# Rows of the attention passes scaled and summed four to a slot

## The chip, the cores and the metric

The kernel runs on one core of a Trainium2 chip. The metric is the device time of one execution. Three runs of the kernel before took 3141.16, 3142.63 and 3146.46 us; the median is 3142.63 us.

## What is computed

A graph has 3125 nodes with 256 features each and 50000 edges, sorted by destination. Four layers follow each other, each added to its input and normalized:

```python
x = _layernorm(x + _L0_gnn_ref(x, src, dst, edge_weight, ...))   # weighted sum over edges, then a two-layer MLP
x = _layernorm(x + _L1_gnn_ref(x, W, att, src, dst))             # attention over edges, 4 heads of 64
x = _layernorm(x + _L2_gnn_ref(x, edge_index, ...))              # two such passes with self loops: 4 heads, then 1 head
x = _layernorm(x + _L3_gnn_ref(x, edge_index, edge_weight, ...)) # dot-product attention over edges, then a feed-forward net
```

In the attention of L1 and L2 every edge gets a logit from its source and its destination; a softmax over the edges of one destination gives weights, and the destination receives the weighted sum of the sources' projected rows:

```python
e = leaky_relu(es[src] + ed[dst])
ex = exp(e - segment_max(e, dst)[dst])
out = segment_sum(ex / segment_sum(ex, dst)[dst] * z[src], dst)
```

## The kernel before

The kernel goes over the edges five times: L0, L1, L2a (the first, four-headed pass of L2), L2b (the second, one-headed pass) and L3. The change is in L1, L2a and L2b, called the attention passes here. An edge pass has 416 steps (STEPS); a step is 128 edges that all end in one block of 128 destination nodes. 16 steps (GS) are a group, and there are 26 groups (NG).

What a step needs, and from which engine:

- GpSimd (POOL) gathers the 128 source rows of a step with an indirect DMA (line 690) into one of 48 ring slots, three groups' worth. The gather of step k waits until the step 48 before it is summed.
- ScalarE (ACT) makes the one-hot matrices M that say which edge goes to which node, four steps at a time (`spread_hots`, lines 2034 and 2038). M has 16 slots, one group's worth, so a batch of four waits until the four steps 16 before it are summed.
- TensorE (PE) picks the destination's part of the logits (`pick`, line 1756), and the group's chain begins.
- VectorE (DVE) multiplies each gathered row by its weights (`scale`, line 1294 with four heads, 1297 with one).
- PE sums the scaled rows into their nodes by a product with M (`sum_step`, line 1806) into one of four PSUM banks.
- DVE adds the bank to the nodes' sums in SBUF (`add`, line 1323). A sum step waits until the add four steps before it has freed its bank.

The chain of a group turns 16 steps of logits into weights. Its parts follow each other across engines: DVE gathers up the picks and makes logits (lines 1174 to 1187), PE turns them (1765), DVE scans them for running maxima (1208, 1212, 1218), PE folds (1772), DVE joins the steps (1232 to 1254), PE fans out (1777, 1784), DVE scans again and subtracts (1264 to 1279), ACT takes the exponential (2021, in `put_alphas`), PE turns it back (1789, in L2a and L2b also 1791), and ACT writes the weights beside the rows (2024). ACT also makes the factor by which old sums fade (`fade_open`, 2012), which DVE applies before a group's first add (1314 and 1317, with one head 1321).

The order is written out by hand. Each engine walks through slots t = 0, 1, 2, ...; group g's chain stands in the 16 slots from 16(g+1) on, called q = 0 to 15 here, so a group's weights are put at q = 14. All engines run their instructions strictly in the order of the program; semaphores make them wait for each other. Step k is scaled by DVE at slot k + 31 (SOFAR), summed by PE at k + 32, and added by DVE at k + 34. So one step of a group is scaled, summed and added in each slot of the next group's chain. In the last two groups of L1 and L2a some of the rows are scaled by ACT and POOL instead (`helper`).

After step SETTLED - 1 = 399 has been added, `scales` and the first blocks of the node work that follows (`early_blocks`) begin between the last adds.

Of the kernel before, what the change touches and what calls it, by code (L numbers as in the profile page):

```python
# [31 lines left out]
STEPS = PADDED + BLOCKS - 1  # L32
SPARTS = STEPS // G
GS = 16
NG = STEPS // GS
WAYS = 4
SOFAR = 31
# [11 lines left out]
SETTLED = TILES - 1 + EARLY  # L49
# [56 lines left out]
def build(nc, x, src, dst, edge_weight, L0_gnn_eps, L0_gnn_w1, L0_gnn_b1, L0_gnn_w2, L0_gnn_b2,  # L106
# [6 lines left out]
    with ctx:  # L113
# [411 lines left out]
        def helper(stage, k):  # L525

            if k < STEPS - HELPED or stage not in ("L1", "L2a"):
                return "vector"
            return ("vector", "scalar", "vector", "pool")[k % 4]

        def scaled_rows(stage, who, k):

            return sum(helper(stage, i) == who for i in range(k + 1))
# [299 lines left out]
        def _(dve):  # L833
# [284 lines left out]
            def residual(t):  # L1118

                if t - 8 not in RESIDUAL_AT:  # L1120
                    return
                b = RESIDUAL_AT.index(t - 8)
                dve.wait_ge(branch_made.sem, branch_made.at("T", b + 1))
                vec.tensor_tensor(at_block(X, b), PS[7][:, D:2 * D], at_block(X, b), ALU.add).then_inc(term_made.sem, 1)
                dve.wait_ge(term_made.sem, term_made.at("T", 2 * b + 1))
                vec.scalar_tensor_tensor(at_block(X, b), bias["bv"][:], at_block(nodeC, b)[:, 1:2], at_block(X, b),
                                         ALU.mult, ALU.add).then_inc(term_made.sem, 1)

            def gat_edges(stage, hops):
# [15 lines left out]
                else:  # L1145
                    ready = norms_of["gat"]
# [141 lines left out]
                def scale(k):  # L1288
                    j = k % RING[stage]
                    if k % GS == 0:  # L1290
                        dve.wait_ge(alphas_put.sem, alphas_put.at(stage, k // GS + 1))
                    if heads > 1:
                        z = ring[:, j, 0:width].rearrange("p (h f) -> p h f", h=heads)
                        ins = vec.tensor_tensor(z, z, ring[:, j, width:width + heads].unsqueeze(2)  # L1294
                                                .to_broadcast([P, heads, width // heads]), ALU.mult)
                    else:
                        ins = vec.tensor_scalar(ring[:, j, 0:width], ring[:, j, 0:width], ring[:, j, width:width + 1],
                                                None, ALU.mult)
                    ins.then_inc(row_scaled.sem, 1)
# [3 lines left out]
                def add(k):  # L1303
                    g, i = divmod(k, GS)
                    if i == 0:
                        blocks[0] = load_blocks(dve, g)
                    if k:
                        dve.wait_ge(sum_added.sem, sum_added.at(stage, k))
                    sums = ACC[:, bass.ds(blocks[0][i], 1), 0:cols].rearrange("p o c -> p (o c)")
                    if i == 0 and g:  # L1310
                        dve.wait_ge(fade_made.sem, fade_made.at(stage, g))
                        if heads > 1:
                            a = sums[:, 0:width].rearrange("p (h f) -> p h f", h=heads)
                            vec.tensor_tensor(a, a, fade[:, 0:heads].unsqueeze(2).to_broadcast([P, heads, width // heads]),
                                              ALU.mult).then_inc(sums_faded.sem, 1)
                            d = sums[:, width:width + heads]
                            vec.tensor_tensor(d, d, fade[:, 0:heads], ALU.mult).then_inc(sums_faded.sem, 1)
                            dve.wait_ge(sums_faded.sem, sums_faded.at(stage, 2 * g))
                    dve.wait_ge(step_summed.sem, step_summed.at(stage, k + 1))
                    if i == 0 and g and heads == 1:  # L1320
                        ins = vec.scalar_tensor_tensor(sums, sums, fade[:, 0:1], PS[k % SUMS[stage]][:, 0:cols], ALU.mult, ALU.add)
                    else:
                        ins = vec.tensor_tensor(sums, sums, PS[k % SUMS[stage]][:, 0:cols], ALU.add)  # L1323
                    ins.then_inc(sum_added.sem, 1)

                early_blocks = slots(0, EARLY, hops) if hops else None
                for t in range(STEPS + SOFAR + 3):
                    g, q = divmod(t - GS, GS)
                    for early in (True, False):
                        if 0 <= g < NG:  # L1330
                            logits(g, q, early)
                            inside(g, q, early)
                            across(g, q, early)
                            peaks(g, q, early)
                        if early and stage == "L3":
                            if 0 <= t - 3 < STEPS:
                                dot(t - 3)
                        elif early and 0 <= t - SOFAR < STEPS and helper(stage, t - SOFAR) == "vector":
                            scale(t - SOFAR)
                    k = t - SOFAR - 3  # L1340
                    if 0 <= k < STEPS:
                        add(k)
                        if hops and k == SETTLED - 1:
                            scales(stage, 0)
                        elif hops and k >= SETTLED:
                            next(early_blocks, None)
                    if stage == "L3":
                        residual(t)
                if hops:
                    finish(early_blocks)  # L1350
# [236 lines left out]
        def _(pe):  # L1587
# [117 lines left out]
            def gat_edges(stage, hops, behind=0):  # L1705
# [101 lines left out]
                        .then_inc(step_summed.sem, 1)  # L1807

                early_blocks = slots(0, EARLY, hops) if hops else None
                for t in range(STEPS + SOFAR + 1):  # L1810
                    g, q = divmod(t - GS, GS)
                    if 0 <= g < NG:
                        turns(g, q)
                    if stage == "L3":
                        if 0 <= t - 2 < STEPS:
                            spread(t - 2)
                    else:
                        for k in (() if q == 2 else (t - 3, t - 2) if q == 3 else (t - 2,)):
                            if 0 <= k < STEPS:
                                pick(k)  # L1820
                    k = t - SOFAR - 1
                    if 0 <= k < STEPS:
                        sum_step(k)
                        if hops and k >= SETTLED + behind:
                            next(early_blocks, None)
                    if stage == "L3":
                        residual(t)
# [145 lines left out]
        def _(act):  # L1973
# [54 lines left out]
            def spread_hots(stage, c):  # L2028

                if c >= 4:  # L2030
                    act.wait_ge(step_summed.sem, step_summed.at(stage, G * (c - 3)))
                here = c % 4 * G
                for i in range(G):
                    last = sc.activation(M[:, here + i, :], iota[:], ACT.Abs, bias=dloc[:, G * c + i:G * c + i + 1], scale=-1.0)  # L2034
                last.then_inc(hot_apart.sem, 1)
                act.wait_ge(hot_apart.sem, hot_apart.at(stage, c + 1))
                quad = M[:, here:here + G, :].rearrange("p i e -> p (i e)")
                sc.activation(quad, quad, ACT.Relu, bias=1.0, scale=-1.0).then_inc(hot_spread.sem, 1)  # L2038

            def gat_edges(stage):  # L2040

                heads, width = HEADS_OF[stage], WIDTH[stage]
                for g in range(NG):
                    spread_hots(stage, 4 * g)
                    spread_hots(stage, 4 * g + 1)
                    if g:
                        fade_open(stage, g)
                    put_alphas(stage, g)
                    spread_hots(stage, 4 * g + 2)
                    spread_hots(stage, 4 * g + 3)  # L2050
                    for k in range(GS * g, GS * (g + 1)):
                        if helper(stage, k) != "scalar":
                            continue
                        j = k % RING[stage]
                        act.wait_ge(alphas_put.sem, alphas_put.at(stage, g + 1))
                        for h in range(heads):
                            z = ring[:, j, h * HID:(h + 1) * HID]
                            last = sc.activation(z, z, ACT.Copy, scale=ring[:, j, width + h:width + h + 1])
                        last.then_inc(act_scaled.sem, 1)
# [230 lines left out]
```

## Time and profile before

| What | Number |
|---|---|
| median of three runs | 3142.63 us |
| span of the profiled execution, first to last instruction | 3624.0 us |
| mean granted TensorE clock in it | 0.719 |
| PE busy | 2348.2 us, 65% |
| DVE busy | 1993.1 us, 55% |
| ACT busy | 1393.5 us, 38% |
| POOL busy | 2222.1 us, 61% |
| chain that ended last: PE / issue / unknown / DVE | 44% / 20% / 14% / 13% |

The profile holds no time around the span, so the span is the profiled execution's own time. It is 481.4 us longer than the median. "Issue" is time in which an engine waited for nothing that the profile shows, "remote" a wait whose end is put down to no instruction of the trace. The first group's chain of L1 begins at about 717 us, that of L2a at 1403, of L2b at 2100; each pass has 26 groups.

### The profile page before, as it was taken

To read this page: it belongs to the slowest core of one execution; us is meant where nothing else is said; L and a number is where in the kernel's file an instruction comes from. 1 tells how busy PE (TensorE), PEld (TensorE's weight loads), DVE (VectorE), ACT (ScalarE), POOL (GpSimd) and SP (SyncE) were. 2 spreads that over 40 slices of the span, in tenths; PEclk is the share of its full clock that TensorE was granted. 3 is DMA by queue.
4 is the path that set the end of the run, shared out by engine and by line. 5 is a ranking of instruction groups with operands and counts; after the bars stand their busy time and mean duration, and the time that the engine had idled before them with its cause. 6 is when DMAs were issued, how large, how long until landed. Compare 5 with 4: busy or idle time off the path is not lost.

```text
span 3624.0 us, 45558 instructions
## 1 busy us (share of the span) xinstructions
PE 2348.2 (65%) x9551; PEld 1619.2 (45%) x9551; DVE 1993.1 (55%) x7394; ACT 1393.5 (38%) x3670; POOL 2222.1 (61%) x2445
## 2 busy tenths in 40 slices
PE   5555557836677763677776624445455578888888
PEld 2323334724344442344444424444444355656567
DVE  5554446536666674566666723333345356666677
ACT  3444544413333343333333413333343144444444
POOL 5666663566667657666766356666654366666636
PEclk8776667956766687666666755555555799999999
DMA  7655664234444423344444022222212255555511
GB/s 201 177 169 167 174 174 135 63 107 114 116 113 116 115 65 109 105 115 115 114 116 112 21 45 45 47 46 47 47 37 71 69 158 155 153 155 158 149 53 49
DMA packets 247934, 389.14 MB, mean 107 GB/s; under 512 B 58944, under 2 KB 161366, under 8 KB 247673
## 3 DMA queue, kind: packets, MB, share of 16 engines
q0 software_dynamic: 92032, 230.64, 24.4%
q1 hardware_dynamic: 155641, 155.59, 14.0%
q8 instruction: 95, 1.56, 0.2%
q14 instruction: 166, 1.36, 0.1%
HBM read 331.11 MB, written 54.91 MB: 107 GB/s over the span
## 4 chain that ended last, share of the span: by engine, by line
PE 44%; issue 20%; another core or an unknown queue 14%; DVE 13%; POOL 3%; ACT 2%; DVEq 2%; DMA 1%; SPq 0%; POOLq 0%; ACTq 0%
PE PS L1806 22%; PE PS L1727 6%; PE PS L1860 4%; PE PS L1698 4%; DVE ACC L1323 3%; POOL work L690 2%; DVE ACC L1090 1%; DVE work L1294 1%; PE PS L1900 1%; PE PS L1784 1%; PE PS L1843 1%; PE PS L1756 1%; DVEq L376 1%; DMA work<-in_x,srcTile 1%
## 5 line engine op out<-in xcount | busy, mean ns | idle before, releaser
L690 POOL DMA_INDIRECT work<-t_z,srcK x1248 | 1224.4, 981 | 614.1 <-issue 299.6
L1806 PE MATMUL PS<-work,M 128*128 128x260 f32 (+3 forms) x3328 | 1279.3, 505 | 470.8 <-issue 238.9
L1806 PEld LDWEIGHTS PS<-work,M 128*128 128x128 f32 x3328 | 744.2, 266 | 691.1 <-issue 486.0
L1323 DVE TENSOR_TENSOR ACC<-ACC,PS 128x260 f32 (+3 forms) x1614 | 588.1, 364 | 217.8 <-PE PS L1806 122.9
L2034 ACT ACTIVATE M<-iota,dloc 128x128 f32<-128x128 f32 x1248 | 396.9, 389 | 667.5 <-PE PS L1806 360.3
L690 POOL DMA_INDIRECT work<-t_x,srcK x416 | 394.3, 948 | 266.3 <-PE PS L1806 139.7
L690 POOL DMA_INDIRECT work<-in_x,srcTile x392 | 375.8, 959 | 210.6 <-issue 106.9
L1698 PE MATMUL PS<-work,M 128*128 x832 | 310.6, 515 | 252.1 <-issue 138.1
L1698 PEld LDWEIGHTS PS<-work,M 128*128 128x128 f32 x832 | 186.4, 249 | 370.2 <-issue 348.0
L1294 DVE TENSOR_TENSOR work<-work 128x256 f32<-128x256 f32 x800 | 328.7, 411 | 18.5 <-issue 11.7
L1756 PE MATMUL PS<-partsD,work 128*128 x1248 | 235.8, 197 | 143.0 <-DVE junk L1174 96.0
L1727 PE MATMUL PS<-Y,w 128*128 x832 | 279.9, 422 | 64.2 <-issue 33.7
L1997 ACT ACTIVATE work<-work,Y 128x256 f32<-128x256 f32 x392 | 183.8, 496 | 268.6 <-DMA work<-in_x,srcTile 191.4
L1756 PEld LDWEIGHTS PS<-partsD,work 128*128 128x128 bf16 x1248 | 179.6, 145 | 228.4 <-issue 174.6
L1090 DVE TENSOR_TENSOR ACC<-ACC,PS 128x256 f32 x416 | 172.9, 416 | 158.0 <-PE PS L1698 52.7
L1199 DVE SCALAR_TENSOR_TENSOR wz<-PS,work 128x258 f32<-128x258 f32 x416 | 173.0, 416 | 150.6 <-PE PS L1727 103.2
L1727 PEld LDWEIGHTS PS<-Y,w 128*128 128x128 f32 x832 | 143.8, 197 | 128.9 <-issue 112.8
L2038 ACT ACTIVATE M<-M 128x512 f32<-128x512 f32 x312 | 196.5, 630 | 10.1
L2074 ACT ACTIVATE work<-work 128x256 f32<-128x256 f32 x416 | 179.4, 494 | 0.1
L579 POOL TENSOR_TENSOR rstd<-variance,minus_half 128x1 f32<-128x1 f32 x125 | 70.9, 579 | 150.9 <-DVE variance L1428 150.9
L2069 ACT ACTIVATE w<-work 128x512 f32<-128x512 bf16 x104 | 65.2, 628 | 227.4 <-PE PS L1727 167.4
L2021 ACT ACTIVATE work<-work 64x128 f32<-64x128 f32 (+1 forms) x104 | 32.1, 309 | 269.8 <-DVE work L1279 155.0
(267 smaller groups left out, 2918.9 us busy)
## 6 DMA issues: line engine op xcount, KB each, us to landing
work<-t_dhot SPq DMA_DIRECT2D x416, 128.0 KB
t_hot<-M SPq DMA_DIRECT2D x104, 256.0 KB
M<-t_hot SPq DMA_DIRECT2D x104, 256.0 KB
work<-t_z,srcK POOLq DMA_INDIRECT x1248
t_dhot<-work SPq DMA_DIRECT2D x104, 128.0 KB
work<-t_edge SPq DMA_DIRECT2D x104, 64.0 KB
work<-t_x,srcK POOLq DMA_INDIRECT x416
t_z<-Y SPq DMA_DIRECT2D x50, 130.0 KB, 1.9
```

The source lines that it names most:

```text
L690: pool.indirect_dma_start(out=slots[:, j, 0:width], out_offset=None, in_=table[:, :], in_offset=bass.IndirectOffsetOnAxis(ap=sources[:, k: ...
L1090: vec.tensor_tensor(a, a, PS[k % 4][:, 0:D], ALU.add).then_inc(sum_added.sem, 1)
L1294: ins = vec.tensor_tensor(z, z, ring[:, j, width:width + heads].unsqueeze(2) .to_broadcast([P, heads, width // heads]), ALU.mult)
L1323: ins = vec.tensor_tensor(sums, sums, PS[k % SUMS[stage]][:, 0:cols], ALU.add)
L1698: mm(PS[k % 4][:, 0:D], M[:, k % (4 * G), :], at_block(rows, places[k % GS])[:, 0:D], start=True, stop=True)\
L1727: mm(PS[3 + k % 2][:, 0:ROWW], dsthotF[c % 2][:, k % G * P:(k % G + 1) * P], at_block(Y, blocks[0][i])[:, 0:ROWW], start=True, stop=True). ...
L1756: mm(PS[4][:, at:at + 3 * heads], dsthot[:, c % 4, k % G * P:(k % G + 1) * P], at_block(partsD, blocks[0][i])[:, 0:3 * heads], start=True, ...
L1806: mm(PS[k % n][:, 0:cols], M[:, k % (4 * G), :], slots_of[:, k % RING[stage], 0:cols], start=True, stop=True)\
L1997: sc.activation(rows[:, j, 0:D], rows[:, j, 0:D], ACT.Copy, scale=wTile[:, t:t + 1]).then_inc(row_scaled.sem, 1)
L2034: last = sc.activation(M[:, here + i, :], iota[:], ACT.Abs, bias=dloc[:, G * c + i:G * c + i + 1], scale=-1.0)
L2038: sc.activation(quad, quad, ACT.Relu, bias=1.0, scale=-1.0).then_inc(hot_spread.sem, 1)
L2074: sc.activation(xring[:, j, 0:D], xring[:, j, 0:D], ACT.Copy, scale=xring[:, j, D:D + 1])\
```

## The change

Three tables (WIDE, NARROW, PACE) give, for each of a group's 16 steps, the slot in which it is scaled, summed and added, counted from the slot after the group's weights are put. All three attention passes are given NARROW (WIDE is defined and not used): steps 0 to 3 are scaled in the first of these slots, 4 to 7 in the second, and so on; the sums come one slot and the adds two slots behind. So DVE's scales stand at q = 15 of the group's own chain and q = 0 to 2 of the next one, PE's sums at q = 0 to 3, DVE's adds at q = 1 to 4. Within a slot DVE alternates between a scale and an add. The slots q = 5 to 14 hold only chain work and picks. ACT makes the third batch of M before the group's weights instead of after them. `scales` begins after step 400's add instead of step 399's. The order of gathers, of picks and of the chain itself is as before, and L3 keeps its pace.

```diff
+        WIDE = {"scale": (0, 0, 0, 0, 1, 1, 1, 2, 2, 2, 3, 5, 7, 9, 11, 13),
+                "sum": (1, 1, 1, 1, 2, 2, 2, 3, 3, 3, 4, 6, 8, 10, 12, 14),
+                "add": (2, 2, 2, 3, 3, 3, 3, 4, 4, 5, 6, 8, 10, 12, 14, 16)}
+        NARROW = {what: tuple(i // 4 + lag for i in range(GS)) for what, lag in (("scale", 0), ("sum", 1), ("add", 2))}
+        PACE = {"L1": NARROW, "L2a": NARROW, "L2b": NARROW}
+        ENDS = GS * (NG + 1) + GS + 8
+
+        def turn_of(stage, what, k):
+
+            g, i = divmod(k, GS)
+            return GS * (g + 2) - 1 + (NARROW if g == NG - 1 else PACE[stage])[what][i]
+
+        def due_at(stage, what, t):
+
+            first = max(0, t // GS - 4) * GS
+            return [k for k in range(first, min(STEPS, first + 5 * GS)) if turn_of(stage, what, k) == t]
...
 # VectorE, gat_edges
-                for t in range(STEPS + SOFAR + 3):
+                def add_and_follow(k):
+                    add(k)
+                    if hops and k == SETTLED:
+                        scales(stage, 0)
+                    if hops and k >= SETTLED:
+                        next(early_blocks, None)
+
+                for t in range(ENDS):
...
-                        elif early and 0 <= t - SOFAR < STEPS and helper(stage, t - SOFAR) == "vector":
-                            scale(t - SOFAR)
-                    k = t - SOFAR - 3
-                    if 0 <= k < STEPS:
-                        add(k)
-                        if hops and k == SETTLED - 1:
-                            scales(stage, 0)
-                        elif hops and k >= SETTLED:
-                            next(early_blocks, None)
+                        elif early:
+                            ready = [k for k in due_at(stage, "scale", t) if helper(stage, k) == "vector"]
+                            summed = due_at(stage, "add", t)
+                            for n in range(max(len(ready), len(summed))):
+                                if n < len(ready):
+                                    scale(ready[n])
+                                if n < len(summed):
+                                    add_and_follow(summed[n])
...
 # TensorE, gat_edges
-                    k = t - SOFAR - 1
-                    if 0 <= k < STEPS:
+                    for k in due_at(stage, "sum", t) if stage != "L3" else [t - SOFAR - 1]:
+                        if not 0 <= k < STEPS:
+                            continue
                         sum_step(k)
...
 # ScalarE, gat_edges
                     spread_hots(stage, 4 * g)
                     spread_hots(stage, 4 * g + 1)
+                    spread_hots(stage, 4 * g + 2)
                     if g:
                         fade_open(stage, g)
                     put_alphas(stage, g)
-                    spread_hots(stage, 4 * g + 2)
                     spread_hots(stage, 4 * g + 3)
```

## Rows read from the trace of the kernel before

**Rows 1.** Windows of L1 and L2b: busy us (count) by engine, granted clock, DMA.

```profile
core 0: us, PE busy (x) PEld busy (x) DVE busy (x) ACT busy (x) POOL busy (x), PEclk, DMA share, GB/s
...
800.00:1300.00 500.00, 356.72 (x1283) 217.56 (x1282) 323.84 (x1090) 176.08 (x489) 343.59 (x344) 0.67 0.42 115
...
2184.00:2674.00 490.00, 242.59 (x1283) 207.59 (x1282) 182.40 (x983) 170.72 (x483) 318.18 (x337) 0.50 0.22 46
```

**Rows 2.** Timeline, DVE: start us, us; chain begin of groups 2 and 24, L1 and L2b.

```profile
798.97 0.35 DVE L1174 TENSOR_REDUCE junk<-PS 128x64 f32<-128x192 f32 x1
...
1312.27 0.36 DVE L1174 TENSOR_REDUCE junk<-PS 128x64 f32<-128x192 f32 x1 [0.51 <-PE PS L1756]
...
2183.47 0.21 DVE L1174 TENSOR_REDUCE junk<-PS 128x16 f32<-128x48 f32 x1
...
2697.19 0.20 DVE L1174 TENSOR_REDUCE junk<-PS 128x16 f32<-128x48 f32 x1
```

**Rows 3.** Windows from group 24's chain begin to group 25's, in L1, L2a, L2b.

```profile
1312.30:1328.10 15.80, 11.78 (x60) 7.18 (x60) 14.68 (x50) 7.89 (x23) 4.58 (x7) 0.98 0.16 39
...
2002.90:2022.80 19.90, 18.04 (x57) 11.01 (x57) 15.25 (x49) 7.53 (x22) 2.68 (x4) 0.50 0.02 8
...
2697.20:2709.40 12.20, 10.63 (x60) 9.58 (x61) 8.51 (x48) 7.37 (x22) 1.43 (x2) 0.50 0.09 18
```

**Rows 4.** Timeline, POOL: gathers in L1, the last two of that pass.

```profile
1312.81 0.97 POOL L690 DMA_INDIRECT work<-t_z,srcK  x1 [0.30 <-issue]
1314.08 0.95 POOL L690 DMA_INDIRECT work<-t_z,srcK  x1 [0.30 <-issue]
```

**Rows 5.** Timeline, DVE, end of L1: add, scale, then a group's first add.

```profile
1309.69 0.41 DVE L1323 TENSOR_TENSOR ACC<-ACC,PS 128x260 f32 x1
1310.02 0.41 DVE L1294 TENSOR_TENSOR work<-work 128x256 f32<-128x256 f32 x1
...
1314.08 0.46 DVE L1314 TENSOR_TENSOR ACC<-ACC,work 128x256 f32 x1 [0.94 <-issue]
...
1314.65 0.42 DVE L1323 TENSOR_TENSOR ACC<-ACC,PS 128x260 f32 x1
```

**Rows 6.** Timeline, PE: two sums at the fast clock, two at the slow clock, L2b's.

```profile
1008.76 1.37 PE L1806 MATMUL PS<-work,M 128*128 128x260 f32 x4
...
1031.04 2.08 PE L1806 MATMUL PS<-work,M 128*128 128x260 f32 x4
...
2461.66 1.10 PE L1806 MATMUL PS<-work,M 128*128 128x66 f32 x4
```

**Rows 7.** Timeline, L1: chain of group 0 (DVE, ACT), then of a later one (PE, ACT).

```profile
734.82 0.41 DVE L1208 TENSOR_TENSOR_SCAN work<-brk,PS 64x128 f32<-64x128 bf16 x1 [0.51 <-issue]
...
736.72 0.35 DVE L1244 TENSOR_TENSOR work<-work,ident 4x128 f32<-4x128 f32 x1
750.26 0.15 DVE L1264 COPY work<-PS 64x2 f32<-64x2 f32 x1 [13.19 <-remote]
...
751.47 0.28 DVE L1279 TENSOR_TENSOR work<-PS,work 64x128 f32<-64x128 f32 x1
...
751.78 0.31 ACT L2021 ACTIVATE work<-work 64x128 f32<-64x128 f32 x1 [39.34 <-issue]
...
1001.31 0.59 PE L1784 MATMUL PS<-work,ones 4*128 4x4 f32 x2
...
1005.17 0.37 PE L1789 MATMUL PS<-ident,work 64*128 64x64 f32 x1
...
1005.58 0.22 ACT L2024 ACTIVATE work<-PS 128x64 f32<-128x64 f32 x1 [1.08 <-PE PS L1789]
1005.70 1.27 ACT L2034 ACTIVATE M<-iota,dloc 128x128 f32<-128x128 f32 x4
1007.00 0.63 ACT L2038 ACTIVATE M<-M 128x512 f32<-128x512 f32 x1
```

**Rows 8.** Timeline, DVE: one add that waited for its sum.

```profile
1024.29 0.43 DVE L1323 TENSOR_TENSOR ACC<-ACC,PS 128x260 f32 x1 [1.98 <-PE PS L1806]
```

More of the change, by code:

```diff
@@ L1337, in gat_edges @@
                                 dot(t - 3)
-                        elif early and 0 <= t - SOFAR < STEPS and helper(stage, t - SOFAR) == "vector":
-                            scale(t - SOFAR)
-                    k = t - SOFAR - 3
-                    if 0 <= k < STEPS:
-                        add(k)
-                        if hops and k == SETTLED - 1:
-                            scales(stage, 0)
-                        elif hops and k >= SETTLED:
-                            next(early_blocks, None)
+                        elif early:
[6 more added lines that the diff above has]
+                                    add_and_follow(summed[n])
                     if stage == "L3":
+                        if 0 <= t - SOFAR - 3 < STEPS:
+                            add(t - SOFAR - 3)
                         residual(t)
@@ L1809, in gat_edges @@
                 early_blocks = slots(0, EARLY, hops) if hops else None
-                for t in range(STEPS + SOFAR + 1):
+                for t in range(ENDS):
                     g, q = divmod(t - GS, GS)
```

## The prediction

> **What bounds the kernel now.** I read the granted clock first, then the busy windows pass by pass, then the waits of POOL, DVE and PE, and last the timeline of single groups.
>
> A group of an attention pass takes the same time whatever is computed in it: from group 2's first chain instruction to group 24's, L1 needs 513.3 us for 22 groups, 23.33 us each, and L2b 513.7 us, 23.35 us each [rows 2], though L2b keeps PE busy for 243 of 490 us and DVE for 182, and L1 PE for 357 and DVE for 324 of 500 [rows 1]. What both share is the gathers. Without waits, one follows the other in L1 after its own duration and 0.30 us [rows 4]; with L1's mean of 343.59 / 344 = 1.00 us that is 1.30 us, 20.8 us for 16, and with L2b's 318.18 / 337 = 0.94 us it is 1.24 us, 19.9 us for 16 [rows 1]. So POOL waits 2.5 us a group in L1 and 3.45 in L2b, for steps that are not summed yet.
>
> The last interval of each pass, in which at most three gathers are left, shows what the other engines need: 15.8 us in L1 at a granted clock of 0.98, 19.9 us in L2a at 0.50, 12.2 us in L2b [rows 3]. Two floors lie below the 23.3 us then: the gather stream, 20.8 or 19.9 us, and the work, 15.8 to 19.9 us with four heads. They are not met because each waits for the other, and because PE's results reach other engines late while gathers stream: DVE's L1264 of group 0 waits 13.19 us though PE has nothing but picks in front of it [rows 7].
>
> **The change, part by part.** No instruction is added or removed in the passes but for their order: 16 scales, 16 sums, 16 adds, 16 gathers, four batches of M a group, as before. What changes is what stands beside what. Today DVE's scales and adds and PE's sums fill the chain's waits. Afterwards they stand together, and the second half of the chain has nothing beside it. So a group of four heads now is a burst followed by a tail.
>
> *Burst, from the weights to L1208.* DVE starts an add or a scale every 0.33 us while nothing is waited for [rows 5]. Nine scales come before the first add: 9 x 0.33 = 3.0 us. In front of a group's first add stand 0.94 us for loading the block numbers, and from L1314's start to the add's end 0.99 us [rows 5]: 1.9 us, so the add ends 4.9 us after the weights. PE has only four banks, so after four sums it waits for this add; sum 4 starts at about 5.1 us. From there DVE and PE run against each other:
>
> - fast clock: a sum takes 1.37 / 2 = 0.69 us [rows 6], less than DVE's share of a step. DVE has 7 more scales, 15 adds and the five logit instructions. The seven scales alternate with adds 1 to 7, 14 x 0.33 = 4.6 us; adds 8 to 15 have no scale between them, and each waits for the one before: 0.42 + 0.03 = 0.45 us, of which the last four come while PE already turns the logits, so 4 x 0.45 = 1.8 us; the logits take some 1.3 us. 4.9 + 4.6 + 1.8 + 1.3 = 12.6 us, and PE has still sums 12 to 15 (they wait for adds 8 to 11), a pick and L1765, 2.2 us: 14.8 us.
> - slow clock: a sum takes 2.08 / 2 = 1.04 us [rows 6]. 5.1 + 12 x 1.04 + 0.6 for three picks and L1765 = 18.2 us.
>
> *Tail, from L1208 to the weights.* Group 0 of L1 has no other work beside its chain: L1208's start to L1244's end 2.25 us, L1264's start to L1279's end 1.49, the exponential 0.34 [rows 7]. L1777 and L1784 between them take twice 0.59, and L1789 to the end of L2024 0.63 us [rows 7]. Sum with the hops between: 6.0 us.
>
> Together 20.8 us at the fast clock and 24.2 at the slow one, against 15.8 and 19.9 us today [rows 3]: 4 to 5 us more, because the tail's 6 us lose their cover. L1 stands now at a mean clock of 0.67 [rows 1], between the levels, so I take the middle, 22.5 us. That is over the gather stream's 20.8, so the work becomes the longer floor.
>
> What comes on top through waits is not shown for this order. It is bounded by what comes on top today: 23.3 - 20.8 = 2.5 us over the longer floor, 23.3 - 17.9 (the middle of 15.8 and 19.9) = 5.4 us over the work. I take 4.0: a group takes 26.5 us, 3.2 us more than now. Ends: 20.8 + 2.5 = 23.3, nothing lost, and 24.2 + 5.4 = 29.6, 6.3 us lost. Over the 52 groups of L1 and L2a: +166 us, from 0 to +328.
>
> *L2b.* A sum takes 1.10 / 2 = 0.55 us at the slow clock [rows 6], scale and add are shorter than with four heads. First add at 3.3 us, then 12 sums, 6.6, and L1765: L1208 at 10.3 us, with the tail 16.3 us, against 12.2 now. Both are under the gathers' 19.9, which is what L2b's 23.35 us stand on. I take no change. Ends: POOL never waits, -3.45 x 26 = -90 us; the wait over the work stays as it is, +4.1 x 26 = +107 us.
>
> *M's third batch before the weights.* A batch takes ACT 1.27 + 0.63 = 1.9 us [rows 7]. It waits for sum 11 of the group before, which comes at 11 to 14 us of the burst, so it is done by 16 us, before the tail needs ACT for `fade_open` and the exponential (4 us after L1208 at the earliest, 18.8 us). Cost nothing; behind it on ACT wait the fade and the weights themselves, so if that cover is gone it is up to 1.9 us a group. The fourth batch, 1.9 us after the weights, is needed by sum 12, at some 11 us: nothing.
>
> *Gathers and loads.* POOL's 16 gathers follow the sums, and are now released within some 12 us instead of over a whole group. The stream cannot be faster than 1.30 us each, so it spreads over the tail. Ring slots stay three groups, so a gather still lands a group or more before it is read: nothing. SyncE's loads for picks are released by picks, whose order stays: nothing. The 32 steps in which ACT and POOL help and the last group of each pass keep their count, three times one group without a chain behind it: 0, within 5 us.
>
> **The sum.** 3624.0 + 166 = 3790 us in the profiled execution's own time. That execution is longer than the median by 481.4 us; carried over in proportion, 3142.6 x 3790 / 3624 = 3287 us. If the waits on top belong to profiled executions alone, a group takes 22.5 us against 23.3 x 3142.6 / 3624 = 20.2 today: +2.3 x 52 = 120, 3262 us. I forecast the middle, 3275 us.
>
> **The clock.** L1's TensorE is busy 71% of the time at a mean clock of 0.67, L2b's 50% at 0.50, that is 1.2 GHz throughout [rows 1]; L1's last interval with 75% stands at 0.98 [rows 3]. The Trainium skill (TensorE: Matmul & The Clock Gate, Part 1: The HAM clock gate) says that sustained matmul activity releases the throttle and idling brings it back, and its section on HAM oscillation warns of gaps in PE's work, after each of which it has to warm up again. By that the dense burst would run at 2.4 GHz after its beginning, and the thin tail, whose matmuls are small, would lose little: it speaks for this change, and is the second rival below.
>
> **The rivals.**
>
> 1. *The burst frees the ring early and nobody waits.* POOL's 16 gathers are released at once, so it streams without waits and sets the time: L1 and L2a at 20.8, L2b at 19.9 us. -2.5 x 52 - 90 = -220 us, in the median's time 2952 us; where half of it comes, 3047. For it: POOL's waits for sums. Against: it needs the fast clock throughout and no late result in the tail. Chance 0.24.
> 2. *The burst warms TensorE.* The work comes down to its fast end, 20.8 us, the waits on top stay at 2.5: 23.3 us, no change, 3143 us. For it: the 0.98 above. Against: four banks let PE idle between sums 3 and 4, and the tail leaves it thin for 6 us. Chance 0.12.
> 3. *Late results meet the banks.* With four banks, sums 4, 8 and 12 each wait for an add that waits for a sum. If each round meets a late result like the add that waited 1.98 us [rows 8], the burst takes 3 x 2 = 6 us more: 312 us on top of the forecast's 166, 4102 us profiled, 3557. Today a step has two slots between sum and add to hide this. It decides where results are late for more than the 0.3 us or so that DVE leaves PE in a round. Chance 0.12.
>
> **How the numbers follow.** The forecast has 0.52; its own ends give 3143 to 3427 us. The range 3000 to 3430 leaves out rival 3 and the fuller part of rival 1. What a measurement here can tell from no change is 0.2%, 3136 to 3149 us. Faster: rival 1 and a little of rival 2, 0.27. The same: rival 2 and the forecast's lower end, 0.08. Slower: 0.65.
>
> **What would show it.** In the trace after, DVE's chain begins (L1174) should lie 25 to 28 us apart in L1 and L2a and about 23 in L2b. DVE should show no scale or add between L1208 and L1279, and idle time before L1232, L1264 and L1294 that grows; PE's sums should stand together, the fifth some 5 us after the weights; POOL should wait longer, once a group. The forecast is wrong if L1's interval is at 23 us or less, if idle time before L1323 inside the burst is what grows (rival 3), or if L2b's interval moves by more than 2 us.

## The result and the profile after

The changed kernel takes 3120.89 us (3119.87 to 3121.85, four runs), the kernel before 3143.76 us beside it: a ratio of 0.9929, 95% interval 0.9915 to 0.9944, so 0.7% or 22.9 us faster. The forecast was 3275 us, slower.

The profiled execution of the changed kernel has a span of 3120.0 us, as long as its runs. That of the kernel before, which the prediction rests on, had 3624.0 us against a median of 3143. Profiled again, the unchanged kernel shows a span of 3136.0 us, and other rows. So three traces stand here side by side: the first one of before (in the prediction's rows), the second one of before, and the one of after. Lines move by 17 to 27 between the kernels: L1174 becomes L1191, the gather L690 becomes L707, the scale L1294 L1311, the add L1323 L1340, the sum L1806 L1832.

Windows of the kernel before, second trace, from group 2's chain begin to group 24's in L1, L2a and L2b (columns as in [rows 1]):

```profile
683.50:1149.30 465.80, 342.92 (x1319) 211.65 (x1320) 331.27 (x1124) 181.52 (x509) 357.35 (x357) 0.71 0.46 128
1300.60:1756.90 456.30, 325.92 (x1345) 200.83 (x1346) 328.23 (x1100) 180.53 (x506) 349.37 (x352) 0.76 0.47 129
1905.70:2346.00 440.30, 243.33 (x1343) 217.72 (x1344) 193.04 (x1035) 177.08 (x507) 333.00 (x353) 0.50 0.25 54
```

The same windows of the changed kernel, its last interval in L1 (which answers to [rows 3]), and one group's burst in L1:

```profile
690.40:1139.20 448.80, 314.56 (x1322) 212.81 (x1320) 362.62 (x1124) 183.15 (x507) 341.61 (x352) 0.76 0.48 131
1292.80:1741.90 449.10, 307.39 (x1344) 199.08 (x1342) 360.19 (x1102) 182.52 (x507) 342.06 (x352) 0.80 0.47 131
1889.80:2330.90 441.10, 225.09 (x1343) 206.89 (x1342) 217.12 (x1036) 176.70 (x507) 333.75 (x353) 0.50 0.25 54
1139.20:1163.70 24.50, 13.67 (x57) 7.90 (x57) 14.64 (x46) 10.83 (x37) 19.16 (x22) 0.73 0.40 104
...
847.32:861.88 14.56, 11.85 (x39) 7.87 (x39) 12.96 (x39) 7.48 (x20) 11.10 (x12) 0.78 0.41 115
```

22 groups each: before 21.17, 20.74 and 20.01 us a group, after 20.40, 20.41 and 20.05. The 23.3 us of [rows 2] are gone from the kernel before as well. These 22 groups of L1 and of L2a gain (0.77 + 0.33) x 22 = 24 us, L2b nothing. PE is busy less and DVE more in the changed kernel, with the same number of instructions to within three.

What sets 20.4 us is POOL. Its gathers in the three windows, grouped by line (columns: line, engine, operation, count | busy us, mean ns of one | idle us before them, by releaser), kernel before, second trace:

```profile
L690 POOL DMA_INDIRECT work<-t_z,srcK x357 | 357.8, 1002 | 108.8 <-issue 81.3 <-PE PS L1806 27.4
L690 POOL DMA_INDIRECT work<-t_z,srcK x352 | 350.8, 997 | 107.2 <-issue 77.4 <-PE PS L1806 29.9
L690 POOL DMA_INDIRECT work<-t_z,srcK x353 | 333.7, 945 | 107.6 <-issue 72.8 <-PE PS L1806 34.8
```

What POOL waited for in the first of these windows (total us, times, longest us):

```profile
POOL work L690 <- issue: 81.3, 267, 0.3
POOL work L690 <- PE PS L1806: 27.4, 90, 0.3
```

The gathers of the changed kernel:

```profile
L707 POOL DMA_INDIRECT work<-t_z,srcK x352 | 342.2, 972 | 107.3 <-issue 74.4 <-PE PS L1832 32.9
L707 POOL DMA_INDIRECT work<-t_z,srcK x352 | 342.7, 974 | 107.3 <-issue 74.1 <-PE PS L1832 33.2
L707 POOL DMA_INDIRECT work<-t_z,srcK x353 | 335.1, 949 | 107.7 <-issue 72.3 <-PE PS L1832 35.4
```

Every idle time of POOL is the 0.30 us that stands between two gathers that wait for nothing [rows 4]: 357 x 0.305 = 108.8 us. Some carry PE's sum as releaser, but none is longer than 0.3 us. So in both kernels POOL gathers without a stop, and a group is 16 x (mean gather + 0.305): 16 x 1.307 = 20.9 us in L1 before, 16 x 1.277 = 20.4 after. (The 21.17 us before are counted between chain begins, L1174, which drift against the gathers: the window holds 357 gathers, not 352. Between the L1178 of the same groups, which wait for a gather, it is 20.92 us.) The gathers became shorter by 0.030 and 0.023 us; over 416 gathers in each of the two passes that is 12.5 + 9.6 = 22 us. That is the gain.

Why would a gather become shorter when only VectorE's order changed? One group of the changed kernel, between two rows of nine scales, shows it. DVE in L1 (start us, us, operation, count):

```profile
847.32 3.10 DVE L1311 TENSOR_TENSOR work<-work 128x256 f32<-128x256 f32 x9 [1.06 <-ACT work L2051]
...
857.38 2.13 DVE L1340 TENSOR_TENSOR ACC<-ACC,PS 128x260 f32 x4
...
859.83 2.13 DVE L1340 TENSOR_TENSOR ACC<-ACC,PS 128x260 f32 x4
861.88 0.41 DVE L1225 TENSOR_TENSOR_SCAN work<-brk,PS 64x128 f32<-64x128 bf16 x1
...
867.83 3.11 DVE L1311 TENSOR_TENSOR work<-work 128x256 f32<-128x256 f32 x9 [1.05 <-ACT work L2051]
870.86 0.42 DVE L1331 TENSOR_TENSOR ACC<-ACC,work 128x256 f32 x1
```

POOL beside it:

```profile
857.86 0.95 POOL L707 DMA_INDIRECT work<-t_z,srcK  x1 [0.30 <-issue]
859.11 0.95 POOL L707 DMA_INDIRECT work<-t_z,srcK  x1 [0.31 <-PE PS L1832]
860.37 0.95 POOL L707 DMA_INDIRECT work<-t_z,srcK  x1 [0.30 <-PE PS L1832]
...
867.89 1.18 POOL L707 DMA_INDIRECT work<-t_z,srcK  x1 [0.30 <-issue]
869.38 1.04 POOL L707 DMA_INDIRECT work<-t_z,srcK  x1 [0.30 <-issue]
870.72 1.04 POOL L707 DMA_INDIRECT work<-t_z,srcK  x1 [0.30 <-PE PS L1832]
```

Beside adds, which read one operand from PSUM, a gather takes 0.95 us; beside the nine scales, both of whose operands lie in SBUF, 1.18, 1.04 and 1.04. In the order before, where a scale stands alone between other work, a gather that meets one or two can be longer still. POOL in L1 of the kernel before, second trace:

```profile
1109.55 0.95 POOL L690 DMA_INDIRECT work<-t_z,srcK  x1 [0.30 <-issue]
1110.80 1.23 POOL L690 DMA_INDIRECT work<-t_z,srcK  x1 [0.30 <-issue]
1112.33 1.28 POOL L690 DMA_INDIRECT work<-t_z,srcK  x1 [0.30 <-PE PS L1806]
```

DVE's scales beside them, and one of the chain's scans, which has both operands in SBUF too:

```profile
1110.79 0.42 DVE L1294 TENSOR_TENSOR work<-work 128x256 f32<-128x256 f32 x1
...
1111.46 0.42 DVE L1294 TENSOR_TENSOR work<-work 128x256 f32<-128x256 f32 x1
...
1112.44 0.41 DVE L1212 TENSOR_TENSOR_SCAN work<-brk,work 64x128 f32<-64x128 bf16 x1
...
1112.77 0.40 DVE L1294 TENSOR_TENSOR work<-work 128x256 f32<-128x256 f32 x1
```

Over L2b's 0.945 us, where the scale has one operand in SBUF and a per-row number, a four-headed scale costs POOL on the mean 1.002 - 0.945 = 0.057 us when spread, and 0.972 - 0.949 = 0.023 us in the burst.

All gathers of the two L1 windows, sorted by what DVE was doing when each began, show more. In the changed kernel the 217 of 352 that begin while no instruction with both inputs in SBUF (a scale, a scan, a fade) is running take 0.948 us, none of them over 0.963; the 135 that begin while one runs take 1.010. In the kernel before 111 of 356 begin while one runs and take 1.094 us: 0.954 where it has under 0.2 us left to run, 1.051 with 0.2 to 0.3 us, 1.179 with more. So the burst does not make fewer gathers begin beside such an instruction; they meet it later in its course (over 0.3 us left for 22 of the 135, for 51 of the 111 before). The other 245 gathers before take 0.961 us; 7% of them are longer than 0.965, up to 1.29 us (the one at 1112.33 us above is such a one), which this sorting does not explain. The experiments test the reading.

### The profile page after: what moved, and what is told of

The parts are those of the page before. It is cut to its first block, busy times and chain, and to the rows that moved or that the text cites. A ratio compares the mean times of both kernels' runs of the same rounds, so it can differ in the third digit from the quotient of the medians.

```text
span 3120.0 us, 45559 instructions
## 1 busy us (share of the span) xinstructions
PE 2179.9 (70%) x9551; PEld 1559.1 (50%) x9551; DVE 2091.6 (67%) x7394; ACT 1393.6 (45%) x3670; POOL 2204.6 (71%) x2445
## 4 chain that ended last, share of the span: by engine, by line
PE 41%; DVE 21%; DMA 13%; POOL 10%; issue 10%; ACT 3%; DVEq 2%; SPq 1%; POOLq 0%; ACTq 0%
PE PS L1832 17%; POOL work L707 9%; DVE ACC L1340 6%; DMA work<-t_z,srcK 5%; PE PS L1887 5%; PE PS L1753 5%; PE PS L1724 4%; DMA work<-in_x,srcTile 4%; DMA t_hot<-M 2%; DMA work<-t_x,srcK 2%; PE PS L1927 1%; PE PS L1810 1%; PE PS L1870 1%; DVE work L1284 1%; DVE work L1290 1%
## 5 line engine op out<-in xcount | busy, mean ns | idle before, releaser
L707 POOL DMA_INDIRECT work<-t_z,srcK x1248 | 1203.7, 964 | 406.1 <-issue 272.9
L1832 PE MATMUL PS<-work,M 128*128 128x260 f32 (+3 forms) x3328 | 1035.9, 450 | 235.1 <-DVE ACC L1340 161.4
L1832 PEld LDWEIGHTS PS<-work,M 128*128 128x128 f32 x3328 | 696.4, 250 | 456.7 <-issue 342.8
L1340 DVE TENSOR_TENSOR ACC<-ACC,PS 128x260 f32 (+3 forms) x1614 | 598.9, 371 | 107.2 <-PE PS L1832 23.9
L707 POOL DMA_INDIRECT work<-t_x,srcK x416 | 396.4, 953 | 127.0 <-issue 94.2
L707 POOL DMA_INDIRECT work<-in_x,srcTile x392 | 376.6, 961 | 135.0 <-issue 80.2
L1724 PEld LDWEIGHTS PS<-work,M 128*128 128x128 f32 x832 | 184.3, 253 | 286.5 <-issue 267.3
L1311 DVE TENSOR_TENSOR work<-work 128x256 f32<-128x256 f32 x800 | 306.7, 424 | 27.5 <-ACT work L2051 26.4
L1753 PE MATMUL PS<-Y,w 128*128 x832 | 266.3, 404 | 28.3 <-DVE wz L1216 20.0
L2039 ACT ACTIVATE work<-PS,group_begins 128x4 f32<-128x4 f32 (+1 forms) x100 | 26.2, 262 | 563.7 <-PE PS L1810 563.7
L1782 PE MATMUL PS<-partsD,work 128*128 x1248 | 149.2, 182 | 64.8 <-DVE junk L1198 23.9
L1195 DVE TENSOR_TENSOR junk<-junk,work 128x64 f32<-128x64 f32 (+1 forms) x78 | 19.1, 245 | 247.6 <-DMA work<-t_z,srcK 247.6
L1092 DVE TENSOR_SCALAR M<-iota,dloc 128x128 f32<-128x128 f32 x416 | 126.0, 304 | 78.6 <-DMA t_hot<-M 74.8
L1782 PEld LDWEIGHTS PS<-partsD,work 128*128 128x128 bf16 x1248 | 113.0, 111 | 118.3 <-issue 90.1
```

The costliest lines, as they stand in the source:

```text
L707: pool.indirect_dma_start(out=slots[:, j, 0:width], out_offset=None, in_=table[:, :], in_offset=bass.IndirectOffsetOnAxis(ap=sources[:, k: ...
L1724: mm(PS[k % 4][:, 0:D], M[:, k % (4 * G), :], at_block(rows, places[k % GS])[:, 0:D], start=True, stop=True)\
L1753: mm(PS[3 + k % 2][:, 0:ROWW], dsthotF[c % 2][:, k % G * P:(k % G + 1) * P], at_block(Y, blocks[0][i])[:, 0:ROWW], start=True, stop=True). ...
L1782: mm(PS[4][:, at:at + 3 * heads], dsthot[:, c % 4, k % G * P:(k % G + 1) * P], at_block(partsD, blocks[0][i])[:, 0:3 * heads], start=True, ...
L1832: mm(PS[k % n][:, 0:cols], M[:, k % (4 * G), :], slots_of[:, k % RING[stage], 0:cols], start=True, stop=True)\
```

## The experiments

**The kernel before, profiled again.** No edit.

> The kernel before, unchanged, profiled again. Theory: the profiled execution that the prediction rests on was itself disturbed (3624 us against a median of 3143), and its late results and stretches with all engines idle are not the kernel's. Then the span is 3135 to 3150 us, the stretches in which PE, DVE and ACT all idle for over 0.25 us vanish from L1 and L2a, and group intervals are some 21 us in L1 and L2a (20.4 of the changed kernel and (3144 - 3121) / 52 = 0.44 us more) and 20.0 to 20.2 us in L2b. Rival: such late results belong to every profiled execution of this order of work, as the changed kernel's has none: span again over 3400 us, intervals again 23.3 us.

Measured: 3137.84 us, span 3136.0, the rows above. The first trace's late results were its own. The waits of DVE in L1 show what the order before does wait for (total us, times, longest):

```profile
DVE junk L1178 <- DMA work<-t_z,srcK: 70.0, 22, 5.5
DVE work L1264 <- PE PS L1784: 31.7, 18, 2.3
DVE ACC L1314 <- issue: 23.5, 22, 1.1
```

It waits for gathers, 70.0 us in 22 groups. L1264, which waited 13.19 us for group 0 in [rows 7], waits 0.7 us there and 2.3 us at the most in these groups.

**Which part of the change.** First, one step a slot in all three passes:

```diff
+        ONES = {what: tuple(i + lag for i in range(GS)) for what, lag in (("scale", 0), ("sum", 1), ("add", 3))}
-        PACE = {"L1": NARROW, "L2a": NARROW, "L2b": NARROW}
+        PACE = {"L1": ONES, "L2a": ONES, "L2b": ONES}
...
-            return GS * (g + 2) - 1 + (NARROW if g == NG - 1 else PACE[stage])[what][i]
+            return GS * (g + 2) - 1 + PACE[stage][what][i]
```

> The changed kernel with a pace of one step a slot in all three attention passes (scale in slot i, sum in i + 1, add in i + 3, as before); ACT's third batch of M ahead of the weights stays, as does the later start of `scales`. If the pace carries the whole gain: 3137 to 3149 us. If the moved batch carries it (a batch that PE's sums wait for in the order before): 3116 to 3126 us.

Measured: 3136.24 us, ratio 0.9998 (0.9988 to 1.0007). The pace carries the whole gain. In the trace, the difference to the changed kernel lies in L1, whose gathers take 1.031 us here; those of L2a take 0.976 us, close to the burst's 0.974 although the scales stand one step a slot. Then one step a slot in the four-headed passes alone (`PACE = {"L1": ONES, "L2a": ONES, "L2b": NARROW}`, last groups as changed):

> The changed kernel with one step a slot in L1 and L2a alone (but for their last group, which keeps four a slot); L2b stays at four a slot. If the gain is made in the four-headed passes, where the intervals are to shrink from about 21 to 20.4 us: 3137 to 3147 us. If L2b makes it: 3117 to 3126 us. Half and half: 3132 us.

Measured: 3133.11 us, 0.9994 (0.9985 to 1.0003); the kernel before took 3135.54 us beside these runs, so the ratios are what compares. Without the four-headed passes nothing measurable is left; the gathers take 1.025 us in L1 and 0.981 in L2a. Last, ACT's third batch of M put back:

```diff
-                    spread_hots(stage, 4 * g + 2)
                     if g:
                         fade_open(stage, g)
                     put_alphas(stage, g)
+                    spread_hots(stage, 4 * g + 2)
```

> The changed kernel with ACT's third batch of M put back behind the group's weights. The prediction costs this edit at nothing: 3115 to 3127 us. Rival: the batch ends 1.9 us after the weights and the fourth 3.8 us after them, and with rows summed in a burst sum 8 meets it, up to 1.9 us a group in the two four-headed passes, less what the gather stream hides: 3130 to 3200 us.

Measured: 3117.79 us, 0.9939 (0.9925 to 0.9952), the changed kernel's 0.9929 within the interval. The edit has no measurable cost or gain.

**The scale's operand.** The weights stand in PSUM before ACT copies them beside the rows. Here `scale` reads them there:

```diff
-                        ins = vec.tensor_tensor(z, z, ring[:, j, width:width + heads].unsqueeze(2)
+                        alpha = PS[6][:, k % GS:GS * heads:GS] if k < STEPS - HELPED else ring[:, j, width:width + heads]
+                        ins = vec.tensor_tensor(z, z, alpha.unsqueeze(2)
...
+                        if heads > 1 and 0 < g <= NG - 2:
+                            pe.wait_ge(row_scaled.sem, row_scaled.at(stage, GS * g))
                         last = nc.tensor.transpose(PS[6][:, 0:R], expd[0:R, :], ident[0:R, 0:R])
```

> The changed kernel, but in L1 and L2a (all groups but the last two) `scale` reads the weights from the PSUM bank into which PE turned them, instead of ACT's copy beside the rows: same 128x256 operation, same count, one operand in SBUF instead of two. Theory: POOL's gather stream alone sets a group, and a gather is longer while a scale with both operands in SBUF runs (0.945 us without one, up to 1.07 with). Then the gathers of L1 and L2a fall from a mean of 0.972 to 0.945 to 0.955 us, their intervals from 20.4 to 20.0 to 20.15 us, and the time to 3096 to 3108 us. Rival: the longer gathers come from their larger rows (1040 bytes against 260 in L2b) or from PE and ACT beside them: mean 0.97, 3116 to 3127 us.

Measured: 3099.56 us, 0.9866 (0.9849 to 0.9883). Its scales in L1, and its gathers in L1 and L2a:

```profile
L1312 DVE TENSOR_TENSOR work<-work,PS 128x256 f32<-128x256 f32 x355 | 131.9, 411 | 23.2 <-ACT work L2054 23.2
...
L707 POOL DMA_INDIRECT work<-t_z,srcK x355 | 337.2, 950 | 108.2 <-issue 78.9 <-PE PS L1835 29.3
...
L707 POOL DMA_INDIRECT work<-t_z,srcK x351 | 333.0, 949 | 107.0 <-issue 73.8 <-PE PS L1835 33.2
```

A scale stays as long as it was (0.41 us), the rows are as large, the order is the same; the gathers fall to L2b's 0.949 us and the groups to 20.07 and 19.99 us. That is the theory's number, and the size of the rows is excluded as the cause. In L1, 108 gathers of the changed kernel begin while a scale runs and take 1.019 us; here 112 begin while a scale, and nothing else with both inputs in SBUF, runs, and they take 0.948. Longer gathers are left only beside other instructions with both inputs in SBUF, as this one, which begins 0.09 us into a scan (first POOL, then DVE):

```profile
1117.84 1.09 POOL L707 DMA_INDIRECT work<-t_z,srcK  x1 [0.30 <-issue]
```

```profile
1117.75 0.42 DVE L1229 TENSOR_TENSOR_SCAN work<-brk,work 64x128 f32<-64x128 bf16 x1
```

The same in the kernel before, for the 12 scales of a group that stand early enough (`if k < STEPS - HELPED and k % GS < 12`), with PE waiting for the twelfth before it writes that bank:

> The kernel before with 12 of 16 scales of a group reading the weights from PSUM in the same way (the other four stand too late in the next chain for that bank), and a wait of PE at L1784's slot for the twelfth of them. Theory of the scales: gathers of L1 and L2a fall from 1.00 to some 0.96 us, intervals from 21.2 and 20.75 to 20.2 to 20.4, the time from 3136 to 3105 to 3118 us: the gain of the change without its order. Rival, the order itself (sums in a burst, steadier clock) makes the gain: 3130 to 3145 us.

Measured: 3118.22 us, 0.9919 (0.9905 to 0.9933); the gathers of L1 take 0.962 us, the groups 20.37 and 20.32. The kernel before gains as much by this edit as by the change, with its order as it was. The expected 3105 to 3118 us stood against 3136 us, ratios of 0.990 to 0.994; the kernel before took 3143.11 us beside this run, and by the ratio the time is as expected. The gathers of L2a, 0.973 us, are longer than the expected 0.96.

**A scale more.** The other way round, in L2b of the kernel before:

```diff
+                        beside = ring[:, j, 66:258]
+                        vec.tensor_tensor(beside, beside, ring[:, j, width:width + 1].to_broadcast([P, 192]), ALU.mult)
                         ins = vec.tensor_scalar(ring[:, j, 0:width], ring[:, j, 0:width], ring[:, j, width:width + 1],
```

> The kernel before with one more VectorE operation a step in L2b, in front of the scale: 128x192 columns of the ring row that L2b doesn't use, multiplied by the weight, both operands in SBUF, no result used. L2b's gathers take 0.945 us on the mean there, and all engines idle for 5.7 us of a group's 20.0. Theory of the scales: gathers of L2b rise to 0.97 to 1.00 us without POOL ever waiting, its interval to 20.4 to 20.9 us, and the time by 10 to 25 us, to 3147 to 3165 us. Rival (size of the gathered rows): gathers stay at 0.945, time within 5 us.

Measured: 3158.28 us, 1.0065 (1.0048 to 1.0082), and L2b's gathers:

```profile
L690 POOL DMA_INDIRECT work<-t_z,srcK x352 | 349.1, 992 | 107.3 <-issue 68.6 <-PE PS L1808 38.7
```

0.945 has become 0.992, the idle time is again 352 x 0.305, a group takes 20.74 us instead of 20.01. An operation whose result nobody uses, on an engine that is busy for 193 of 440 us there without it, makes the kernel some 20 us slower through POOL.

**How dense a burst.** Two steps a slot in L1 and L2a (`i // 2 + lag`):

> The changed kernel with two steps a slot in L1 and L2a instead of four (last group and L2b unchanged). Theory of the scales: what counts is how many gathers a scale meets; with scales spread over eight slots instead of four the mean gather lies between 0.972 and 1.00 us, 3122 to 3134 us. Rival: any burst that lets the chain stand free does: 3114 to 3122 us.

Measured: 3120.71 us, 0.9929 (0.9913 to 0.9945), gathers 0.976 and 0.972 us. The theory expected something in between and failed here; the rival's time was met, two a slot do as well as four. The way is the same, shorter gathers. In L1 138 of 353 begin while an instruction with both inputs in SBUF runs, as many as with four a slot, and take 1.023 us: how short gathers get is not simply a matter of the number of slots over which the scales are spread.

**The work under the stream.** To see what the orders need by themselves, every second gather of the attention passes was left out from the fourth group on, in the kernel before and in the changed one (`if not fetched(stage, k): continue`, and the waits count the gathers that come).

> The kernel before with every second gather of the three attention passes left out from their fourth group on (the rows left from earlier steps are used in their place, so the results are others; scales, sums, adds and the chain keep their count). POOL's stream is then some 10 us a group and no longer the bound, so the interval shows the work of this order. The forecast put it at 15.8 us at the fast clock and 19.9 at the slow one: L1 and L2a 15.8 to 19.9 us a group, L2b some 12 us. If the work were the bound in the whole kernel too, they stay at 21 and 20 us.

> The changed kernel with the same gathers left out. The forecast put burst and tail at 20.8 us at the fast clock and 24.2 at the slow one for L1 and L2a, 16.3 us for L2b: if that was right and only hidden by the gather stream, intervals stay at 19.5 to 21 us in L1 and L2a while the order before falls to 16 to 19 us, and the changed kernel becomes the slower of the two. If the burst costs nothing: 16 to 18 us like the order before.

Measured, one execution each: 2742.73 and 2954.47 us. Windows of the kernel before without them, group 2 to 24 of L1 and of L2b:

```profile
690.00:1058.80 368.80, 303.70 (x1321) 182.90 (x1322) 324.75 (x1124) 180.87 (x508) 189.25 (x187) 0.85 0.36 100
1696.40:1967.20 270.80, 240.96 (x1343) 217.66 (x1344) 188.68 (x1035) 177.16 (x507) 179.84 (x190) 0.50 0.30 67
```

And of the changed kernel:

```profile
692.00:1125.70 433.70, 304.61 (x1322) 203.66 (x1320) 360.22 (x1124) 182.88 (x507) 180.51 (x186) 0.80 0.31 85
1853.60:2177.30 323.70, 223.46 (x1342) 205.98 (x1342) 213.77 (x1036) 176.65 (x506) 178.97 (x190) 0.50 0.24 56
```

What POOL waited for in the first of these two (total us, times, longest us):

```profile
POOL work L714 <- PE PS L1839: 227.1, 137, 8.2
```

POOL now waits for sums, and the groups show the work: 16.8 us against 19.7 in L1, 12.3 against 14.7 in L2b (L2a: 16.2 against 19.9). Freed from the stream, the changed order is the slower one by 212 us. Its work lies 0.5 to 0.7 us a group under the stream of 20.4 us, which hides it.

**The end of a pass.** The last interval of L1 takes 24.5 us after the change; in the second trace of before it takes 15.8. One step a slot for the last two groups (`ONES if g >= NG - 2`):

> The changed kernel with the last two groups of each attention pass at one step a slot again. The interval of the last full group, behind the end of the gather stream, was 15.8 and 19.1 us in the order before and is 24.5 us in the changed one. If that end lies on the path by itself: 5 to 8 us less in L1 and L2a each, 3105 to 3114 us. If the end of the stream sets it whatever the order: 3117 to 3125 us.

Measured: 3118.92 us, 0.9922 (0.9909 to 0.9936). The interval falls to 16.0 us, but from L1's last gather to L2a's first one the trace gains only 71.4 - 67.2 = 4.2 us (the kernel before, second trace: 70.1), and the ratio cannot be told from 0.9929. The expectation of 5 to 8 us for each pass failed. Together with the weights from PSUM:

> The changed kernel with the weights read from PSUM and the last two groups of each pass at one step a slot: 3100 us less the 4 us or so by which that end shortened the stretch from a pass's last gather to the next pass's first one in L1 and in L2a (71.5 to 67.2 and 72.7 to 68.7 us): 3088 to 3097 us. If the two do not add up: 3097 to 3104 us.

Measured: 3092.84 us, 0.9859 (0.9842 to 0.9875), the lowest time of the kernels that gather every row. It is faster than the end's edit alone (0.9922); against the 0.9866 of the weights from PSUM alone it is not a measured difference, so whether the two add up stays open (the kernel before was 6 us faster beside this run than beside those two).

## Why the prediction was wrong

- **"What comes on top through waits ... I take 4.0."** This is the step that failed: nothing came on top. A group of the changed kernel in L1 is POOL's gathers one after another, 16 x 1.277 = 20.4 us, where 26.5 were forecast. The 23.3 us a group, POOL's 2.5 us of waiting and the late results of [rows 7] belonged to that one profiled execution. In an execution of the usual length a group of L1 takes 21.17 us and POOL never waits. Four of the 26.5 us forecast were carried over from a disturbed trace. The prediction saw that the execution was 481 us longer and priced the case that the waits belong to it, at 3262 us; that case, without the 4.0, failed by the next step, which put 22.5 us of work where 19.7 were measured.
- **"That is over the gather stream's 20.8, so the work becomes the longer floor."** The work at the fast clock was worked out nearly right: 15.8 us for the order before (16.8 in L1 and 16.2 in L2a measured with half the gathers, at mean clocks of 0.85 and 0.91), 20.8 for the new one (19.7 and 19.9 measured, at 0.80 and 0.78). Burst and tail can be read in the trace: from the first scale at 847.32 us to L1225 at 861.88 us 14.6 us (forecast 14.8), from there to the next group's first scale at 867.83 us 6.0 us (forecast 6.0). The burst's agreement is partly luck: the 0.94 us for the block numbers did not show, so the first add ended 4.0 us after the first scale and not 4.9, while adds without scales between them came 0.57 us apart and not 0.45, and 0.6 us went into waiting for a gather. But the middle between the two clocks was the wrong choice: this burst took the fast clock's time at a mean granted clock of 0.78. At 19.7 us the work stays just under the stream, and the 3 us that it grew cost nothing.
- **"The stream cannot be faster than 1.30 us each."** It could: 1.307 became 1.277 us, and 1.255 with the weights in PSUM. The row for it was at hand: L2b's gathers of 0.94 us against L1's 1.00 in [rows 1], which the disturbed trace shows as the second one does, and which the prediction used as two given numbers and did not ask about. The gain by way of shorter gathers stands in none of its rivals.
- **Rival 1** named the state (POOL streams and sets the time) and 20.8 us for L1; 20.4 was measured. Its price of -220 us was wrong, since POOL streamed before the change too. **Rival 2** fell: the granted clock rose from 0.71 to 0.76 in L1 (in L2a, from 0.76 to 0.80, other traces of the two orders overlap), but with the stream as the bound that moves nothing. **Rival 3** fell: in L1 of the changed kernel PE's sums wait 2.3 us for adds in all 22 groups together.
- **L2b unchanged**, and **M's third batch at nothing**: right in what they forecast (20.01 to 20.05 us; 0.9939 against 0.9929), though L2b's 23.35 us and POOL's waits in it were the disturbed trace's.

The Trainium skill (SBUF — State Buffer, Who interferes with whom) says that a VectorE instruction with two inputs in SBUF contends with a GpSimd instruction that reads SBUF. The gathers agree if they count as such a reader: in the changed order 0.972 us on the mean with both inputs of the scales in SBUF, 0.950 with one in PSUM. The same section says that in a probe `tensor_tensor` did not stall a DMA, and infers as the reason that descriptor generation needs the write interface alone; here the gathers got longer beside it, and the measurement decides.

**What stays open.** A gather is longer when it begins while such an instruction runs, and the more so the longer that still runs; one that begins later in the gather costs nothing in the changed kernel. In the kernel before, the gather at 1109.55 us above, which has a scale from 1109.88 us on, takes 0.95 us, and the one at 1110.80 us, with a scale at its very start, 1.23. Why the start of a gather decides is not shown, nor what made the 7% longer. What sets the point at which gathers meet scales is only in part shown. In the dense row a longer gather and its gap take 1.34 us (from 869.38 to 870.72), as long as four scales of 0.335, so the next gather meets its scale at the same point, with little left to run. With four or two steps a slot the mean gathers of L1 and L2a lie between 0.968 and 0.976 us in all traces; with one step a slot they lie anywhere from 0.976 (L2a, the experiment with one step in all passes) to 1.031 us (L1, the same), and what sets them there was not tried. What disturbed the first profiled execution was not found; none of the later traces shows it. An extra VectorE operation of the same size with one SBUF operand in L2b was not tried.

## What to carry to other kernels

Compare the profiled span with the runs before reading an interval from it; where it is 15% too long, look for a stretch whose length can be worked out from durations alone (16 gathers x 1.25 us) and trust that. When an engine runs without waits, ask what makes its own instructions longer in one stage than in another: the 0.06 us by which gathers differed between L1 and L2b is worth some 45 us over the 832 gathers of two passes, twice what the change brought. And a reordering that costs 3 us of work in each group can still gain, as long as the work stays under the stream that bounds it.

## What was not expected of the hardware

A VectorE multiplication with both operands in SBUF (128x256, 0.42 us) lengthens an indirect gather of POOL that begins while it runs from 0.95 to as much as 1.23 us in the rows shown, though the two work on different rows and neither waits for the other by a semaphore; the same multiplication with one operand in PSUM does not (0.948 us for 112 gathers in L1). Where no such instruction runs at its start, a gather of 128 rows takes POOL 0.95 us + 0.30 us whether the rows have 260 bytes (L2b) or 1040 (L1).
